# A graph network kernel: nodes laid out by tiles, the count-times-bias term on TensorE, x's statistics first, two of three parts on GpSimd

## The reference

```python
h = relu(layernorm(x))                                   # layer 0
ef = (relu(ea @ We1 + be1) @ We2 + be2) * sigmoid(ew * Wt + bt)
msg = relu(concat(h[src], ef) @ Wn1 + bn1) @ Wn2 + bn2
x = x + h + segment_sum(msg, dst)
h = relu(layernorm(x))                                   # layer 1
a = h + segment_sum(h[src], dst)
x = x + relu(relu(a @ W1 + b1) @ W2 + b2)
```

## Time and profile before

| | us |
|---|---|
| median of 3 runs | 3589.09 |
| lowest and highest of them | 3583.87, 3596.16 |
| the profiled execution, device time | 3590.76 |
| its span in the trace | 3589.0 |

### The profile page before, as it was taken

The page is one execution under the profiler, slowest core; times in us unless marked ns, Lnnn a source line. Parts: engine busy times, 40 slices in busy tenths (PEclk is TensorE's granted clock), DMA queues, the critical chain, the costliest instruction groups (busy, mean ns, idle before and its releaser), DMA issues.

```text
span 3589.0 us, 51735 instructions
## 1 busy us (share of the span) xinstructions
PE 2681.7 (75%) x14584; PEld 1614.4 (45%) x14585; DVE 1962.9 (55%) x4112; ACT 1004.6 (28%) x1000; POOL 2068.4 (58%) x2104
## 2 busy tenths in 40 slices
PE   4688878788777877788777877877745767666777
PEld 2444444444444444444434443433432544544554
DVE  7655655566565666566656666665763333233333
ACT  3233333333333333333333332322231111011111
POOL 4666666666566656666666566655324556555552
PEclk8788888788887887888888888888865766767778
DMA  5444444444343444344343443433222434334332
GB/s 188 110 124 134 130 132 126 128 127 135 121 127 122 126 122 123 121 126 123 122 124 124 122 123 121 124 106 118 48 94 84 152 99 129 104 111 126 117 103 62
DMA packets 229412, 426.77 MB, mean 119 GB/s; under 512 B 82703, under 2 KB 141584, under 8 KB 229072
## 3 DMA queue, kind: packets, MB, share of 16 engines
q0 software_dynamic: 74752, 153.23, 16.3%
q1 hardware_dynamic: 103152, 177.42, 15.0%
q10 hardware_dynamic: 51266, 93.34, 7.4%
HBM read 364.35 MB, written 59.43 MB: 118 GB/s over the span
## 4 chain that ended last, share of the span: by engine, by line
PE 41%; issue 20%; DVE 17%; another core or an unknown queue 11%; DVEq 9%; DMA 1%; SPq 0%; ACT 0%; ACTq 0%
PE ps L891 9%; PE ps L803 9%; PE ps L762 8%; PE ps L771 5%; DVE nodes L1152 5%; PE ps L782 4%; PE ps L754 3%; DVEq L1086 2%; DVEq L1132 2%; DVE arena L1152 2%; DVE hot L1107 1%; PE ps L881 1%; DVE acc L1094 1%; DVEq L1149 1%
## 5 line engine op out<-in xcount | busy, mean ns | idle before, releaser
L525 POOL DMA_INDIRECT big<-table,idx x2080 | 2044.2, 983 | 1391.8 <-issue 588.2
L803 PE MATMUL ps<-nodes 128*128 128x500 bf16 x1280 | 461.1, 476 | 348.7 <-issue 200.0
L762 PE MATMUL ps<-arena,we 128*128 128x512 f32 x784 | 516.4, 791 | 18.5 <-issue 13.3
L611 ACT ACTIVATE big<-big 128x1024 f32<-128x1024 f32 x196 | 207.1, 1057 | 1072.0 <-DVE big L1101 932.0
L782 PE MATMUL ps<-hot,big 128*128 128x64 f32 x3136 | 391.3, 274 | 99.4 <-issue 67.2
L1152 DVE TENSOR_SCALAR nodes<-iota_k,win_off,nodes 128x500 bf16<-128x500 f16 x1280 | 453.0, 405 | 0.0
L782 PEld LDWEIGHTS ps<-hot,big 128*128 128x128 f32 x3136 | 378.0, 194 | 102.2 <-issue 100.1
L1149 DVE TENSOR_TENSOR nodes<-iota_b,nodes 128x384 bf16<-128x384 f16 (+1 forms) x492 | 244.8, 497 | 278.6 <-remote 156.9
L803 PEld LDWEIGHTS ps<-nodes 128*128 128x128 bf16 x1280 | 107.6, 106 | 589.1 <-issue 308.0
L1101 DVE TENSOR_TENSOR big<-ps,big 128x1024 f32<-128x1024 f32 x196 | 239.0, 1219 | 225.5 <-issue 217.6
L601 ACT ACTIVATE arena<-ps,cols 128x1024 f32<-128x1024 f32 x196 | 218.6, 1115 | 405.3 <-PE ps L754 222.3
(11 more groups left out here) (139 smaller groups left out, 2512.4 us busy)
## 6 DMA issues: line engine op xcount, KB each, us to landing
arena<-in_ew SPq DMA_DIRECT2D x196, 512.0 KB
arena<-in_ea SPq DMA_DIRECT2D x196, 256.0 KB
counts_d<-arena ACTq DMA_DIRECT2D x192, 245.0 KB
acc<-counts_d ACTq DMA_DIRECT2D x15, 2940.0 KB
big<-table,idx POOLq DMA_INDIRECT x2080
table<-big SPq DMA_DIRECT2D x7, 672.0 KB, 3.0
idx<-in_src SPq DMA_DIRECT2D x260, 4.0 KB
xs<-in_x SPq DMA_DIRECT2D x7, 448.0 KB, 8.7
```

Of the source, the lines that this page charges most:

```text
L525: pool.indirect_dma_start(to(u, q, t), None, table, bass.IndirectOffsetOnAxis(ap=idx[:, u, at:at + 1], axis=0))\
L762: pe.matmul(p_ef[q], we2[:, :], hid[:, q, :], start=True, stop=True).then_inc(ef_mm, 1)
L803: m = pe.matmul(to, hots[:, t, :], keys[:, t, :], start=False, stop=True, skip_group_check=True)
```

## The change

The node layout becomes one by tiles: tile t holds the nodes 128t to 128t+127. `acc_group`, both tables, the loads of x and the stores of the result follow, and so does the split of a source number (L1162 to L1171: now division by 128, with the same number of instructions). A group of `acc` is now an unbroken run of columns; the loads of x, the stores of `table0` and the stores of the result move pieces of 512 bytes, the stores of `table1` pieces of 768 bytes.

The prologue loads x first and takes its statistics first; the minimum and maximum come behind them, SP queues the first four pairs ahead of the small results, POOL adds the normalized x to x, and DVE works out the loop parameters behind step g = 5 of its loop. The bias stage has no copy of the counts, no copies by ACT and no DVE bias: PE adds a product of one row, counts by bn2, in the same accumulation. SP loads the stored counts behind all seven products. In the parts stage POOL makes the first and the second part, DVE makes the remainder of group g and then the third part of group g-1, and its seven copies to `acc` follow as a loop of their own. The gathers of padding tiles read 16 rows in place of 128, five in each gather stage.

```diff
+            x_tiles, out_tiles = (a.rearrange("p c -> (p c)").rearrange("(t p d) -> p t d", p=P, d=D) for a in (x, out))
             for g in range(NG):
                 sp.dma_start(xs[:, g * GT:(g + 1) * GT, :],
-                             x[:, g * GT * D:(g + 1) * GT * D].rearrange("p (t d) -> p t d", d=D))\
+                             x_tiles[:, g * GT:(g + 1) * GT, :])\
                   .then_inc(x_loaded[g], 16)
+            sp.dma_start(dst_b, dst_blocks).then_inc(dst_loaded, 16)
+            sp.dma_start(dst_t[:, :], dst_tiles).then_inc(dst_tiles_loaded, 16)
...
-            v = acc[:, which, 0:N_PAD].rearrange("f (p t) -> f t p", t=NT)
+            v = acc[:, which, 0:N_PAD].rearrange("f (t p) -> f t p", p=P)
...
-            t1 = table1.rearrange("(p t) d -> p t d", t=NT)
+            t1 = table1.rearrange("(t p) d -> p t d", p=P)
...
-            sp.dma_start(count_n[:, :], acc[0:1, 1, 0:N_PAD].rearrange("a (p t) -> a p t", t=NT)).then_inc(counts_moved, 16)
-            sp.wait_ge(counts_moved, 16)
+            sp.wait_ge(upd_mm, NG)
             for i in (0, 1):
                 sp.wait_ge(c_stored[i], 16 + 16 * (NW0 // 2))
             load_sums(sp, 0)
...
+            for g in range(NG):
+                x_g = xs[:, g * GT:(g + 1) * GT, :]
+                pool.wait_ge(normed, g + 1)
+                pool.tensor_tensor(x_g, x_g, stages[g % 2], ALU.add).then_inc(xh_made, 1)
+            def gather_block(table, to, u, q, landed, n=TB):
                 for t in range(TB):
                     at = q * TB + t
+                    rows_of = slice(0, P if t < n else 16)
...
-            for g in range(NG):
-                pool.wait_ge(left_made, g + 1)
-                pool.tensor_copy(parts[:, g % 2, :, 1, :], left).then_inc(parts_second, 1)
+            for g in range(NG + 1):
+                if g < NG:
+                    pool.wait_ge(normed1, g + 1)
+                    if g >= 2:
+                        pool.wait_ge(table1_stored[g % 2], 16 * (g // 2))
+                    pool.tensor_copy(parts[:, g % 2, :, 0, :], nodes[:, g * GT:(g + 1) * GT, :]).then_inc(parts_first, 1)
+                if g >= 1:
+                    pool.wait_ge(left_made, g)
+                    pool.tensor_copy(parts[:, (g - 1) % 2, :, 1, :], lefts[(g - 1) % 2]).then_inc(parts_second, 1)
...
-                act.activation(stages[g % 2], acc_group(g), ACT.Copy).then_inc(acc_staged, 1)
...
-                act.activation(parts[:, g % 2, :, 0, :], nodes[:, g * GT:(g + 1) * GT, :], ACT.Copy).then_inc(parts_first, 1)
...
+                sums, edges = acc_group(g), acc_group(g, 1)
                 for u in range(GT):
-                    i = pe.matmul(p_prod[g % 2][:, u, :], stages[g % 2][:, u, :], wn2[:, :], start=True, stop=True)
+                    pe.matmul(p_prod[g % 2][:, u, :], sums[:, u, :], wn2[:, :], start=True, stop=False)
+                    i = pe.matmul(p_prod[g % 2][:, u, :], edges[0:1, u, :], bn2_r[0:1, :], start=False, stop=True)
...
-            add_bias(0)
             for g in range(NG):
                 x_g = xs[:, g * GT:(g + 1) * GT, :]
                 dve.wait_ge(upd_mm, g + 1)
-                dve.wait_ge(x1_chain, g + 1)
                 dve.tensor_tensor(x_g, x_g, p_prod[g % 2], ALU.add).then_inc(x1_made, 1)
-                if g < NG - 1:
-                    add_bias(g + 1)
...
+            for g in range(NG + 1):
+                if g < NG:
+                    dve.wait_ge(parts_first, g + 1)
+                    if g >= 2:
+                        dve.wait_ge(parts_made, g - 1)
+                    dve.tensor_tensor(lefts[g % 2], nodes[:, g * GT:(g + 1) * GT, :], parts[:, g % 2, :, 0, :], ALU.subtract)\
+                       .then_inc(left_made, 1)
+                m = g - 1
+                if m >= 0:
+                    dve.wait_ge(parts_second, m + 1)
+                    dve.tensor_tensor(parts[:, m % 2, :, 2, :], lefts[m % 2], parts[:, m % 2, :, 1, :], ALU.subtract)\
+                       .then_inc(parts_made, 1)
             for g in range(NG):
-                dve.wait_ge(parts_first, g + 1)
-                if g:
-                    dve.wait_ge(parts_made, g)
-                dve.tensor_tensor(left, nodes[:, g * GT:(g + 1) * GT, :], parts[:, g % 2, :, 0, :], ALU.subtract)\
-                   .then_inc(left_made, 1)
                 dve.wait_ge(turned1, g + 1)
                 dve.tensor_copy(acc_group(g), p_turn[g % 2]).then_inc(acc1_made, 1)
-                dve.wait_ge(parts_second, g + 1)
-                dve.tensor_tensor(parts[:, g % 2, :, 2, :], left, parts[:, g % 2, :, 1, :], ALU.subtract)\
-                   .then_inc(parts_made, 1)
```

More of the change, by code:

```diff
@@ L435, in _ @@
                   .then_inc(tile_ends_loaded, 16)
+            sp.wait_ge(sweeps_made, 1)
+            sweeps, start, total, bodies = load_params(sp)
             for b in range(1, NBODY):
@@ L532, in gather_pair, with gather_rest @@
                     gather_block(table, to, u, q, landed)
+            def gather_rest(table, to, u, q, landed):
+                gather_block(table, to, u, q, landed, EDGE_TILES - (NTILE - (2 - q) * TB))
             def to_rows(u, q, t):
@@ L543, in _, with gather_body @@
                 gather_pair(table0, to_rows, u, gathered)
[L545 removed]
+            def gather_body(b, last=False):
                 for u in range(RING):
@@ L550, in gather_body @@
                     pool.sem_inc(pairs_begun, 1)
-                    gather_block(table0, to_rows, u, 0, gathered)
+                    gather = gather_rest if last and u == RING - 1 else gather_block
+                    gather(table0, to_rows, u, 0, gathered)
                     pool.wait_ge(agg_mm, b * RING + (u - 2))
                     pool.sem_inc(pairs_begun, 1)
-                    gather_block(table0, to_rows, u, 1, gathered)
+                    gather(table0, to_rows, u, 1, gathered)
             for b in range(1, NBODY):
-                gather_body(b)
+                gather_body(b, b == NBODY - 1)
+            pool.wait_ge(sweeps_made, 1)
+            sweeps, start, total, bodies = load_params(pool)
             with pool.If(sweeps > 1):
@@ L1031, in _ @@
                 if g < NG:
-                    x_g = xs[:, g * GT:(g + 1) * GT, :]
-                    dve.wait_ge(normed, g + 1)
-                    dve.tensor_tensor(x_g, x_g, stages[g % 2], ALU.add).then_inc(xh_made, 1)
                     dve.wait_ge(turned, g + 1)
@@ L1257, in _ @@
                     sweep(s, False)
-            dve.wait_ge(counts_moved, 16)
-            def add_bias(g):
-                for t in range(g * GT, (g + 1) * GT):
-                    i = dve.scalar_tensor_tensor(out=xs[:, t, :], in0=bn2_r[:, :], scalar=count_n[:, t:t + 1],
-                                                 in1=xs[:, t, :], op0=ALU.mult, op1=ALU.add)
-                i.then_inc(x1_chain, 1)
-            add_bias(0)
             for g in range(NG):
```

151 lines of the change are left out of this document (73 added, 78 removed).

## The result

The changed kernel takes 3651.13 us (median of five runs; four lie between 3640.65 and 3651.58, and the fifth, 3712.53 at a granted clock of 0.658, was disturbed and counts in no ratio), the kernel before 3589.09: a ratio of 1.0155 with a 95% interval of 1.0128 to 1.0182. A later set on another chip gave 1.0139 (1.0112 to 1.0166). The forecast was 3587 with a range of 3574 to 3600: wrong, and on the side to which it gave 0.14.

A forecast was written before the change was run, and what follows sets the result against it. No engine was held full in the rewritten stages; chains of waits and single engines set their pace. Terms -9.3 + 0 - 5.3 + 23.1 - 10.3 = -1.8; 3590.8 - 1.8 - 1.7 = 3587 us, range 3574 to 3600.

The forecast's parts named there:

- The bias stage: From last sums to shift: one-row product priced like 128-row ones, 27.4 us for seven groups; stage -5.3 us.
- clock low throughout, 7 x 5.75: Upper bound of the bias stage: every group's 28 instructions at PE's low clock, +7.6 us.
- Rival 2: Bias stage: PE's clock stays low, costing 12.9 us, total 3600; chance 0.08.
- 0.11 of "faster": Share of the forecast's chance below 3578.3 us, where the bias stage nears its lower bound of -15.
- The prologue: Up to the last nodes: x and its statistics first, scale and shift at 16.7 us; booked -9.3 us.
- The bound of 19.5: Prologue: latest time in us for scale and shift, with x at two thirds of the rate for 512-byte pieces.
- The parts stage: Shift to first gather of second stage: one store between any two third parts, period 7.2 us; +23.1 us.
- Rival 5: Parts stage: release order misread, period stays 3.9 us a group; about 16 us less, total 3571; chance 0.06.
- The last stage: Products with W1: unbroken columns instead of a step of 49 elements speed up PE; -10.3 us.
- rival 4: Last stage: the column step is not what makes L937 slow, stage unchanged, total 3597; chance 0.06.
- The gather stages: First booked 0, at most -1 us; second moves with its first gather, or 3.9 us more by PE's own start.
- Rival 3: Small pieces cost double: stores +1.4 us in five periods, 6 us lost in the prologue, total 3601; chance 0.06.

The follow-up runs named there:

- b_full: Changed kernel with the bias product over all 128 rows instead of row 0 alone: bias stage 31.1 us, ratio to the kernel before 0.9984.
- b_group: Changed kernel with each group's seven one-row bias products placed behind its seven sums products: bias stage 43.7 us.
- b_g128: Changed kernel with each group's seven bias products behind its seven sums products and over all 128 rows: bias stage 31.0 us.
- b_none: Changed kernel with the product of counts and bias left out: bias stage 25.1 us, ratio to the kernel before 0.9987.
- p_two: Changed kernel with GpSimd making both its parts of a group in a row, VectorE its three operations likewise, two buffers: parts stage 36.6 us.
- best2: Changed kernel with 128-row bias product, three reordered part buffers, early slots, need-ordered loads, sweep parameters last: 2863.60 us against 2892.13 for the kernel before, ratio 0.990.

## Why the prediction was wrong

**The bias stage: the step that failed.** "The one-row product has no row. It streams the same 128 columns", priced by a row of like instructions. With that price the forecast of 32.6 us from the last sums to the shift is right for 128 rows (31.1 in b_full) and wrong by 44 for one row. The term mis-sized is 28 instructions a group: 3.6 us forecast, 10.13 measured, 3.13 a group with all rows. I bounded it by "clock low throughout, 7 x 5.75", taking the low clock as the worst that can happen, and so the bound itself lacked a mechanism: what two neighbours of unlike row counts do to each other. That costs about 0.30 us at each of 14 changes in a group, 29 us in all by the estimate above, and nobody named it. Rival 2 named the rest, the clock, at 0.08, and priced it at 12.9 where the same estimate gives 16; that b_group and b_g128 lie 12.7 apart does not confirm its price, since they differ in more than the clock. The stage was also the place of the widest downward tail I gave, 0.11 of "faster", which stood on DVE being the bound: true in b_none, at 25.1, which has no bias product.

**The prologue**, -9.3 forecast, -2.8 measured. The shift came at 18.6 instead of 16.7: x in 512-byte pieces moves at 298 GB/s (share 1.20) where its 3,584-byte pieces, with the destinations', moved at 390 at 1.02. The bound of 19.5 had foreseen that, and the value should have been nearer to it. The wait for the sixteenth load of parameters (PE at 24.9, ACT standing 2.5) was not in the working at all: these loads stand behind x's and the destinations' on SP, which had issued both at 6.6 us before and at 10.8 now. The last four of x's seven loads take about 1.5 us each to issue; before, the median of the seven was 0.52 and one took 1.6. The parameters of the sweeps took 4.9 for 3.7, as the first ran beside GpSimd's addition, and the last product behind them (L750) took 3.36 at a granted clock of 0.50, where 1.8 was forecast and 1.73 is what the ones before it took. Along the chain that is 1.9 for the shift, 2.2 until the parameters start, 1.2 for them and 1.5 behind them, 6.8 in all; the 0.3 booked for the last store lies outside the stage, and 6.5 is the miss. GpSimd's addition took 2.10 (1.9 forecast) and showed nowhere else.

**The parts stage** was right in mechanism and size: period 7.16 for 7.2 (store 3.25, cast 0.95, remainder 1.79, third part 1.01, against 3.3, 0.94, 2.03, 0.93), first gather 57.3 behind the shift for 58.0. p_two shows the cause: the same instructions and buffers in another order of GpSimd's queue take 36.6. Rival 5's figure, 16 less, was too small, since p_two also takes the copies off the end.

**The last stage** was right: L949 takes 1.02 where L937 took 1.98, -9.3 for -10.3; rival 4 falls. **The gather stages**, in the profile: the first -1.7 for 0. The second came out 13 longer, more than the 3.9 allowed for, without a cause found in its own instructions. The forecast had no term for how much these stages differ from profile to profile.

**The sum.** 44.1 + 6.5 + 13.0 - 1.7 - 0.7 + 1.0 is 62, the distance of the profiled span from the forecast one (3649.3 against 3587.2); by medians it is 64. With the bias stage as forecast the time would have come to about 3607 by this median, still above the range. (Rival 3's own terms, 7 and 6 us, make 3600 and not 3601, which changes no chance.) The gains booked for the prologue and the last stage are real, and best2 shows what they are worth once the one-row product and the queue order are mended.

## What to carry to other kernels

A small product put between large ones is not priced by its columns: look for a row in which neighbours of unlike row counts alternate, and where there is none, give the term an upper bound well above "the same at the low clock", or, where the missing rows are zeros that are there anyway, use them all: that took 45 us off here. When a queue takes on a second step, write the releases of both steps out over two rounds; here the buffers lost their overlap with no instruction added. A layout that cuts a transfer into 512-byte pieces also delays what is queued behind it (the destinations' loads were issued 4.2 us later here), and the wait to look for is the one for the last small load.

## What the runs showed of the hardware

- Fp32 products of 128 rows and of 1 or 32 rows in alternation take 0.36 us an instruction at the low clock, whether the small one adds onto the large one's place in PSUM or goes to another bank (1 row); grouped by row count (1 row) 0.235; all of 128 rows at the full clock 0.11 from start to start. With one-row products in half of the instructions, grouped, the granted clock was 0.55 over the first 32.4 us; with 128 rows in the same order it was 0.52 over the first 6.8 us and 0.99 from there on:

```profile
2625.60:2658.00 32.40, 32.19 (x149) 30.19 (x150) 11.13 (x33) 0.00 (x0) 2.80 (x1) 0.55 0.01 2
```
```profile
2101.80:2108.60 6.80, 5.75 (x28) 5.78 (x29) 0.00 (x0) 0.00 (x0) 2.81 (x1) 0.52 0.02 5
2108.60:2132.80 24.20, 18.95 (x170) 18.76 (x169) 19.90 (x67) 0.25 (x1) 0.00 (x0) 0.99 0.17 56
```

- The same program takes 2888 us on one chip and 3596 on another (profiled spans), with every stage outside the gathers within 1 us. In the first gather stage the instructions are the same in number; PE is busy 1806 against 1995 us and the clock is 0.93 against 0.83:

```profile
54.90:2106.60 2051.70, 1805.96 (x9700) 1067.04 (x9700) 1575.44 (x3001) 829.55 (x781) 1533.92 (x1568) 0.93 0.50 150
```
```profile
55.60:2600.30 2544.70, 1994.87 (x9700) 1120.75 (x9700) 1563.43 (x3001) 836.48 (x782) 1550.32 (x1568) 0.83 0.41 121
```

  PE's own work is longer by 189 of the 493 us; the rest is idle time, and its cause was not looked for. A ratio of one chip is not that of another: 28 us are 1.0% of the one and 0.8% of the other.
- Loads in 512-byte pieces ran at 298 GB/s with the DMA share at 1.20, against 390 GB/s at 1.02 in long ones. The Trainium skill's page DMA: Bandwidth & Descriptors, section Specifications, has 512 bytes as the size from which the full rate is reached. This case doesn't agree for plain loads (298 against 390); for the stores of 768-byte pieces the loss was 0.25 us in 3.0.
